# The first chunk of a selective scan, set up by TensorE and VectorE together and evicted tile by tile

## What is computed

```python
def _L1_attn_ref(x, in_proj_w, conv_w, conv_b, x_proj_w, dt_proj_w, dt_proj_b, A_log, D_param, out_proj_w):
    x_in, res = jnp.split(jnp.einsum('bld,ed->ble', x, in_proj_w), 2, axis=-1)
    xp = jnp.pad(x_in, ((0, 0), (K_CONV - 1, 0), (0, 0)))
    conv = conv_b
    for k in range(K_CONV):                                  # 4 taps
        conv = conv + xp[:, k:k + seqlen, :] * conv_w[:, k]
    u = _silu(conv)                                          # 512 channels
    dt_in, Bm, Cm = jnp.split(jnp.einsum('bld,ed->ble', u, x_proj_w), [64, 80], axis=-1)
    dt = jax.nn.softplus(jnp.einsum('blr,er->ble', dt_in, dt_proj_w) + dt_proj_b)
    A = -jnp.exp(A_log)                                      # 512 channels x 16 states
    def step(h, t):
        dt_t, B_t, C_t, u_t = t
        h = jnp.exp(dt_t[:, :, None] * A) * h + (dt_t * u_t)[:, :, None] * B_t[:, None, :]
        return (h, jnp.einsum('bdn,bn->bd', h, C_t))
    ...
    y = (jnp.swapaxes(ys, 0, 1) + u * D_param) * _silu(res)
    return jnp.einsum('blr,or->blo', y, out_proj_w)
```

## Time and profile before

| what | value |
|---|---|
| three runs, median (lowest to highest) | 3345.03 us (3344.44 to 3349.97) |
| the profiled execution's own time | 3345.35 us |
| its span in the trace | 3343.5 us |
| mean granted TensorE clock over the span | 0.966 of full speed |
| TensorE / VectorE / ScalarE / GpSimd busy, share of the span | 90% / 79% / 67% / 67% |
| preparation of chunk 0, from the first instruction of the scan stage to its first scan | 1580.9 to 1625.8 us |

### The profile page before, as it was taken

One profiled execution on the slowest core, in us unless ns is written; L12 is line 12 of the kernel. 1 busy time (PEld: TensorE's weight loads), 2 busy tenths in 40 slices (PEclk: granted clock), 3 DMA queues, 4 the chain that ended last, 5 costly groups with the idle time before them and its releaser, 6 DMA issues. The chain is left out here.

```text
span 3343.5 us, 39386 instructions
## 1 busy us (share of the span) xinstructions
PE 3017.1 (90%) x11504; PEld 1711.8 (51%) x11504; DVE 2644.0 (79%) x3513; ACT 2232.7 (67%) x3411; POOL 2227.2 (67%) x1615
## 2 busy tenths in 40 slices
PE   3589999999999999999889999999988899999997
PEld 1157666666666667777334434433433444444432
DVE  5989989898989898555699999999999444555543
ACT  2457676766767666665566666666564788888886
POOL 3578888888888888776367767776786344444443
PEclk7689999999999999999899999999999999999999
DMA  3034444444444444455122222222321222222222
GB/s 98 13 93 133 125 131 126 120 134 124 125 132 126 122 124 126 142 147 155 48 73 70 73 70 71 72 70 70 92 69 54 90 97 96 103 102 103 102 102 90
DMA packets 199617, 335.38 MB, mean 100 GB/s; under 512 B 21379, under 2 KB 57380, under 8 KB 199020
## 3 DMA queue, kind: packets, MB, share of 16 engines
q1 hardware_dynamic: 199404, 332.86, 32.9%
HBM read 325.69 MB, written 7.09 MB: 100 GB/s over the span
## 5 line engine op out<-in xcount | busy, mean ns | idle before, releaser
L1639 POOL TENSOR_TENSOR c_hc<-c_h,c_c_rep 128x1024 f32<-128x1024 f32 x256 | 604.1, 2360 | 277.0 <-DVE c_h L1681 216.2
L1681 DVE TENSOR_TENSOR_SCAN c_h<-c_decay,c_carry,c_v_ps 128x512 f32<-128x512 f32 x512 | 638.9, 1295 | 0.4 <-DVE c_v_ps L1671 0.4
L2133 POOL TENSOR_TENSOR d_acc<-d_acc,d_prod 128x512 f32<-128x512 f32 x240 | 311.6, 1308 | 421.3 <-DVE d_prod L2201 421.1
L1539 ACT ACTIVATE c_decay<-c_dt,c_a_cols 128x512 f32<-128x512 f32 x512 | 364.0, 721 | 339.2 <-DVE c_h L1681 337.8
L2093 ACT ACTIVATE d_hmid<-d_up,n_b 128x1024 f32<-128x1024 f32 x512 | 532.4, 1118 | 84.9 <-PE d_up L1995 84.7
L1387 PE MATMUL c_y_ps<-c_hc,ident 128*128 128x512 f32 x1024 | 499.2, 611 | 43.5 <-POOL c_hc L1639 31.7
L687 POOL TENSOR_TENSOR ab_inner_low<-ab_inner,ab_inner_high 128x512 fp32r<-128x512 f32 x264 | 341.9, 1295 | 241.1 <-ACT ab_inner_high L570 239.8
L559 ACT ACTIVATE ab_gate_ps<-ab_gate_ps,ab_raw_d 128x512 f32<-128x512 f32 x264 | 174.5, 661 | 430.8 <-PE ab_gate_ps L414 430.7
L2201 DVE SCALAR_TENSOR_TENSOR d_prod<-d_ring,n_b,d_w_rep 128x512 f32<-128x512 f32 x240 | 180.2, 751 | 280.6 <-PE d_ring L2005 145.7
L669 POOL TENSOR_TENSOR ab_hc<-ab_h,ab_c_rep 128x512 f32<-128x512 f32 x256 | 331.8, 1296 | 86.7 <-DVE ab_h L740 65.7
L675 POOL TENSOR_TENSOR ab_gu_low<-ab_raw_gu,ab_gu_high 128x512 fp32r<-128x512 f32 x264 | 341.7, 1294 | 4.3 <-ACT ab_gu_high L546 4.3
(11 more groups left out here) (280 smaller groups left out, 6405.3 us busy)
## 6 DMA issues: line engine op xcount, KB each, us to landing
ab_raw_gu<-in_b_experts SPq DMA_DIRECT2D x264, 256.0 KB, 3.4
ab_w_rep<-ab_w_scratch SPq DMA_DIRECT2D x264, 256.0 KB, 3.6
c_c_rep<-c_c_scratch SPq DMA_DIRECT2D x256, 256.0 KB, 3.1
d_w_rep<-d_w_scratch SPq DMA_DIRECT2D x256, 256.0 KB
ab_raw_d<-in_b_experts SPq DMA_DIRECT2D x264, 129.0 KB, 2.1
ab_raw_x<-in_xT SPq DMA_DIRECT2D x32, 256.0 KB, 4.8
out<-xT SPq DMA_DIRECT2D x8, 512.0 KB, 10.1
xT<-in_xT SPq DMA_DIRECT2D x1, 3072.0 KB, 12.3
```

Source lines behind the costliest of these rows:

```text
L1539: nc.scalar.activation(decay[:, i % DEC, :], dt[:, s, m, :], ACT.Exp, scale=a_cols[:, n * NM + m:n * NM + m + 1]).then_inc(decay_ready, 1)
L1639: nc.gpsimd.tensor_tensor(hc[:, q % HC], h[:, q % HR], c_rep[:, q % BC].unsqueeze(1).broadcast_to([P, PAIR, CH]), ALU.mult).then_inc(hc_re ...
L1681: nc.vector.tensor_tensor_scan(out=h[:, q % HR, m, :], data0=decay[:, i % DEC, :], data1=v_ps[m][:], initial=carry[:, i:i + 1], op0=ALU.mu ...
L2133: nc.gpsimd.tensor_tensor(acc[:, s, g, :], acc[:, s, g, :], prod[:, q % PR, :], ALU.add).then_inc(add_ready, 1)
```

## The change

Only the preparation of chunk 0 is changed, and what the loops need because of it.

- The four projected tiles come in the order 2, 3, 0, 1 and go to four banks (both `v_ps`, `bank_a`, `bank_b`); ScalarE copies each to `xin` as it comes.
- Tiles 2 and 3 are convolved by VectorE in SBUF, straight into `u`: one `tensor_scalar` and three `scalar_tensor_tensor` for each tile, the two tiles alternating, each operation waiting by a semaphore for the one before it on its tile. Tiles 0 and 1 are convolved by TensorE into both `y_ps`. So six banks are in use. The diagonals of tiles 0 and 1 are made first, those of tiles 2 and 3, which chunk 1 is the first to need, after the constants; TensorE's `convolve` of chunk 1 waits for them at tile 2.
- Silu is applied tile by tile, with the convolution's bias: to `u` for tiles 2 and 3, straight from PSUM for 0 and 1. The matmuls of `project_u` follow tile by tile.
- A Softplus of one column into a new tile `spare` comes right behind the last Silu.
- x_dbl is copied before `b_parts`. The four matmuls of dt go to four banks, with no wait between them; Softplus is applied to each straight from PSUM, with its bias.
- The halo copy comes last on ScalarE. After it ScalarE waits for the spare Softplus, the constants (now six) and its own four Softplus, raises five semaphores that the loops count on, and begins the decays.
- VectorE's `dtu` waits for the first two Softplus and the four Silus; the first product waits for all four Softplus.

```diff
             pe.wait_ge(loaded, LOADS)
             pe.sem_inc(y_ready, HC)
+            for n, m in enumerate(FIRST_ORDER):
+                first_x(n, m)
+            pe.wait_ge(diag_ready, 1)
+            for n in range(PAIR):
+                first_convolve(n)
+            first_u()
             for m in range(NM):
-                project_x(0, m)
+                first_dt(m)
             pe.wait_ge(const_ready, CONSTS)
-            for m in range(NM):
-                convolve(0, m, (0, 1, 2, 3))
-            project_u(0, 0, (0, 1, 2, 3))
-            for m in range(NM):
-                project_dt(0, m)
             spread_b(0, 0, 0)
...
+            def first_u():
+                pe.wait_ge(x_left, NM)
+                for n, m in enumerate(FIRST_ORDER):
+                    pe.wait_ge(first_u_ready, n + 1)
+                    done = nc.tensor.matmul(bank_b[:], x_w[:, m, :], u[:, 0, m, :],
+                                            start=(n == 0), stop=(n == NM - 1))
+                done.then_inc(xd_ready, 1)
...
+            act.wait_ge(halo_ready, 1)
+            for n, m in enumerate(FIRST_ORDER):
+                act.wait_ge(x_ready, n + 1)
+                nc.scalar.copy(xin[:, m, HALO:], (v_ps[0], v_ps[1], bank_a, bank_b)[n][:]).then_inc(x_left, 1)
+            for n, m in enumerate(FIRST_ORDER):
+                if n < PAIR:
+                    act.wait_ge(first_cv, n + 1)
+                    src = u[:, 0, m, :]
+                else:
+                    act.wait_ge(cv_ready, n - PAIR + 1)
+                    src = y_ps[m][:]
+                nc.scalar.activation(u[:, 0, m, :], src, ACT.Silu, bias=conv_b[:, m:m + 1]).then_inc(first_u_ready, 1)
+            nc.scalar.activation(spare[:, 0:1], conv_b[:, 0:1], ACT.Softplus).then_inc(spare_ready, 1)
+            act.wait_ge(xd_ready, 1)
+            nc.scalar.copy(x_dbl[:], bank_b[:]).then_inc(xd_left, 1)
+            nc.scalar.copy(b_parts[RANK:, 0, :], bank_b[RANK:, :]).then_inc(xd_left, 1)
             for m in range(NM):
-                leave_x(0, m)
+                act.wait_ge(dtp_ready, m + 1)
+                nc.scalar.activation(dt[:, 0, m, :], (v_ps[0], v_ps[1], bank_a, bank_b)[m][:], ACT.Softplus,
+                                     bias=dt_b[:, m:m + 1]).then_inc(dt_half_ready, 1)
+            nc.scalar.copy(xin[:, :, 0:HALO], xin[:, :, CH:CH + HALO]).then_inc(halo_ready, 1)
+            act.wait_ge(spare_ready, 1)
             act.wait_ge(const_ready, CONSTS)
-            for m in range(NM):
-                leave_conv(0, 0, m)
-            keep_halo(0)
-            activate_u(0, 0)
-            leave_x_dbl(0, 0)
-            leave_dt(0, 0, 0)
...
-            softplus(0, 0, 0, 1)
-            softplus(0, 0, 1, 1)
+            act.wait_ge(dt_half_ready, NM)
+            act.sem_inc(dt_ready, PAIRS)
+            act.sem_inc(dtp_left, NM)
+            act.sem_inc(cv_left, NM)
+            act.sem_inc(cv_ready, PAIR)
+            act.sem_inc(u_ready, 1)
...
+            def first_convolve():
+                dve.wait_ge(halo_ready, 1)
+                dve.wait_ge(x_left, PAIR)
+                for j in range(TAPS):
+                    for m in FIRST_ORDER[:PAIR]:
+                        at = FIRST_ORDER.index(m)
+                        if j == 0:
+                            nc.vector.tensor_scalar(u[:, 0, m, :], xin[:, m, 0:CH], conv_w[:, m, 0:1], None,
+                                                    ALU.mult).then_inc(first_step[at], 1)
+                        else:
+                            dve.wait_ge(first_step[at], j)
+                            nc.vector.scalar_tensor_tensor(
+                                out=u[:, 0, m, :], in0=xin[:, m, j:j + CH], scalar=conv_w[:, m, j:j + 1],
+                                in1=u[:, 0, m, :], op0=ALU.mult, op1=ALU.add
+                            ).then_inc(first_cv if j == TAPS - 1 else first_step[at], 1)
...
             nc.vector.memset(xin[:, :, 0:HALO], 0.0).then_inc(halo_ready, 1)
+            diagonals((0, 1)).then_inc(diag_ready, 1)
             nc.vector.memset(carry[:], 0.0).then_inc(const_ready, 1)
...
+            first_convolve()
             nc.vector.memset(b_parts[0:RANK].bitcast(F32), 0.0).then_inc(const_ready, 1)
...
             nc.vector.tensor_scalar(a_cols[:], a_cols[:], -1.0, None, ALU.mult).then_inc(const_ready, 1)
+            diagonals((2, 3)).then_inc(diag_ready, 1)
             dve.wait_ge(const_ready, CONSTS)
...
             nx.place_embedding(dve)
-            first_input()
+            ms = slice(0, PAIR)
+            dve.wait_ge(dt_half_ready, PAIR)
+            dve.wait_ge(first_u_ready, NM)
+            nc.vector.tensor_tensor(dtu[:, ms], dt[:, 0, ms], u[:, 0, ms], ALU.mult).then_inc(dtu_ready, 1)
+            dve.wait_ge(dt_half_ready, NM)
```

More of the change, by code:

```diff
@@ L1177, in layer1_scan @@
         carry = sb("carry", [P, NT])
+        spare = sb("spare", [P, 8])
         z = sb("z", [P, 2, CH])
@@ L1191, in layer1_scan @@
         const_ready = sem("const_ready")
+        diag_ready = sem("diag_ready")
+        first_cv = sem("first_cv")
+        first_u_ready = sem("first_u_ready")
+        first_step = [sem(f"first_step{i}") for i in range(PAIR)]
         x_ready = sem("x_ready")
@@ L1284, in convolve @@
                 if taps[0] == 0:
+                    if is_int(r, 1) and m == 2:
+                        pe.wait_ge(diag_ready, 2)
                     if m < 2:
@@ L1437, in chunk, with first_x, first_convolve, first_dt @@
                         add_states(c, q - 2)
+            def first_x(n, m):
+                out = (v_ps[0], v_ps[1], bank_a, bank_b)[n]
+                for half in range(2):
+                    done = nc.tensor.matmul(out[:], in_w[:, half, m * P:(m + 1) * P], xT[:, half, 0:CH],
+                                            start=(half == 0), stop=(half == 1))
+                done.then_inc(x_ready, 1)
+            def first_convolve(m):
+                pe.wait_ge(x_left, PAIR + m + 1)
+                for j in range(TAPS):
+                    done = nc.tensor.matmul(y_ps[m][:], conv_diag[:, m, j, :], xin[:, m, j:j + CH],
+                                            start=(j == 0), stop=(j == TAPS - 1))
+                done.then_inc(cv_ready, 1)
+            def first_u():
[5 more added lines that the diff above has]
+                done.then_inc(xd_ready, 1)
+            def first_dt(m):
+                if m == 0:
+                    pe.wait_ge(xd_left, 2)
+                out = (v_ps[0], v_ps[1], bank_a, bank_b)[m]
+                nc.tensor.matmul(out[:], dt_w[:, m * P:(m + 1) * P], x_dbl[0:RANK, :],
+                                 start=True, stop=True).then_inc(dtp_ready, 1)
             pe.wait_ge(loaded, LOADS)
             pe.sem_inc(y_ready, HC)
+            for n, m in enumerate(FIRST_ORDER):
[4 more added lines that the diff above has]
+            first_u()
             for m in range(NM):
-                project_x(0, m)
+                first_dt(m)
             pe.wait_ge(const_ready, CONSTS)
-            for m in range(NM):
-                convolve(0, m, (0, 1, 2, 3))
-            project_u(0, 0, (0, 1, 2, 3))
-            for m in range(NM):
-                project_dt(0, m)
             spread_b(0, 0, 0)
@@ L1741, in chunk, with diagonals @@
                     scan(c, q, 1)
+            def diagonals(ms):
+                for m in ms:
+                    for j in range(TAPS):
+                        done = nc.vector.tensor_scalar(conv_diag[:, m, j, :], k["ident"], conv_w[:, m, j:j + 1], None,
+                                                       ALU.mult)
+                return done
+            def first_convolve():
+                dve.wait_ge(halo_ready, 1)
+                dve.wait_ge(x_left, PAIR)
+                for j in range(TAPS):
+                    for m in FIRST_ORDER[:PAIR]:
[9 more added lines that the diff above has]
+                            ).then_inc(first_cv if j == TAPS - 1 else first_step[at], 1)
             dve.wait_ge(loaded, LOADS)
             nc.vector.memset(xin[:, :, 0:HALO], 0.0).then_inc(halo_ready, 1)
+            diagonals((0, 1)).then_inc(diag_ready, 1)
             nc.vector.memset(carry[:], 0.0).then_inc(const_ready, 1)
[L1746 to L1749, removed]
-            done.then_inc(const_ready, 1)
+            first_convolve()
             nc.vector.memset(b_parts[0:RANK].bitcast(F32), 0.0).then_inc(const_ready, 1)
```

13 lines of the change are left out of this document (4 added, 9 removed).

## The result

The changed kernel took 3328.3 us (median of five runs, 3327.86 to 3330.16), the kernel before 3349.97 us over five runs beside it (3344.44 to 3360.31). The ratio on record is 0.9939, with a 95% interval of 0.9924 to 0.9954; it is an estimate from the runs and not the quotient of the two medians, which is 0.9935. Two of the five runs of the kernel before, at 3360.1 and 3360.3, stand 10 us or more above the other three, so the difference of these two medians, 21.7 us, is more than the profiles bear out. The profiled execution took 3327.86 us, 17.5 us less than that of before (3345.35). It holds all three numbers that the case turns on: where the first scan starts, how long the stage runs from there, and how long the last stage takes.

The account below looks back on a forecast made before the run. VectorE bounds the scan stage but idles 28.58 us before it, behind a ScalarE and TensorE chain. Bringing the first scan 18.6 us earlier takes 3345.35 to 3326.7 (3326.4 from the median); forecast 3326.5 us, range 3323 to 3331.

Parts of the forecast that it names:

- TensorE up to x_dbl: Chunk 0's preparation, projections through two convolutions and x_w: x_dbl copied at 1598.6 instead of 1614.49, 15.9 us earlier.
- Beside it: Work beside TensorE before x_dbl: VectorE's convolution 4.8 us, Silu load and Silus, constants, embedding; Silus ready in time, costing nothing.
- The rival that VectorE becomes the bound: VectorE's eight convolution operations each expose a 0.49 us semaphore round trip: 2.1 us less gained, 3328.6 us; chance 10%.
- dt and the tail: From x_dbl to the first scan: Softplus done at 1604.3, then 0.8 and 2.1 us; first scan 1607.2, 18.6 us earlier.
- the clock rival: TensorE's clock falls to 0.50 after its pause between x_w and dt: 3.4 us lost, 3330 us; chance 10%.
- The tail of 0.8 us: ScalarE after the last Softplus: halo copy 0.2 us, three waits and five semaphore counts 0.6 us (bounds 0 to 1.0).
- The table loads: ScalarE's function-table loads take 1.28 us each without a drain; two off the chain are worth 2.56 of the 18.6 us.
- Moves with it: From the first scan on, VectorE never lacks work, so stage end and what follows come earlier by as much.
- The slower rival: TensorE stays behind through all 256 scan steps, 0.12 us each costing 29 us, net 3356 us; chance 2%.
- The base: Kernel before: the sum used its profiled execution, 3345.35 us, 0.3 us above the median of three runs, 3345.03.

Follow-up runs that it names:

- pe_all: Changed kernel with all four tiles of chunk 0 convolved by TensorE into four banks, all diagonals made first; 3340.79 us, single profiled execution.
- split_consts: Kernel before, with TensorE's convolutions waiting for the diagonals alone and the other constants waited for later; 3342.14 us, single profiled execution.
- u_late: Changed kernel with TensorE's x_w waiting for all four Silus before its first matmul; 3332.25 us, single profiled execution.
- dve_serial: Changed kernel with VectorE convolving tile 2 wholly, then tile 3, instead of alternating; 3327.47 us, single profiled execution.
- no_spare: Changed kernel without the one-column spare Softplus and the wait for it; 3327.84 us, single profiled execution.
- leave_early: Changed kernel with ScalarE copying chunk 1's projected tiles in chunk 0's steps 1, 3, 5, 7 instead of 5 to 8; 3332.61 us, single profiled execution.
- again: Changed kernel measured once more with no edit; median 3331.99 us, ratio 0.9956 to the kernel before.
- again2: Changed kernel measured a third time with no edit; median 3329.63 us, ratio 0.9945 to the kernel before.

## Why the prediction was right

The forecast was 3326.5 us, range 3323 to 3331, and 3328.3 was measured; the gain between the profiled executions was forecast at 18.6 us and was 17.5. The mechanism came as forecast: the first scan starts earlier by what the chain up to it loses, 17.83 us for a forecast 18.6, and the rest moves with it. That the total came within 1.8 us is in part luck, as the same code had medians of 3328.3, 3332.0 and 3329.6 in three comparisons, of which 3332.0 lies outside the range. Nor is the first scan at 1607.48, forecast at 1607.2, as close as it looks: from the stage's start it was 27.03 for 26.3.

- **TensorE up to x_dbl.** Forecast 17.7 us after the stage's start, measured 17.61 or 17.62 in all ten profiles that leave this part as it is. Against the first copy before, at 33.57, that is 15.96 us (forecast 15.9). Parts of it were taken out one by one: two convolutions 6.87 (pe_all), the wait for constants 2.3 and part of the clock 0.87 (split_consts), the order of x_w 1.1 (u_late). About 4.8 us are left, of which the rest of x_w's slow clock is 1.6 (x_w to its copy takes 3.63 instead of 6.08); the remainder, Silu tile by tile out of PSUM and no eviction or halo between, is argued, as no run undoes it alone.
- **Beside it.** VectorE's 4.8 us were 4.86, the Silu load started straight behind the last copy. VectorE's wait ahead of `dtu`, forecast at 1 us, was gone, as one group of eight small casts took 1.72 us where its like took 0.73 before; the room behind it bore that. The rival that VectorE becomes the bound fell with dve_serial.
- **dt and the tail.** This is the step that was mis-sized. The first Softplus was at 20.01 (forecast 20.1), the last started at 23.73 instead of 22.7: the clock rival, priced at 3.4 us for a fall ahead of dt, came true in part, in the middle of it, and cost 1.14. I had given it 10%; in ten profiles with the pause unaltered it was there in five, so 10% was far too little. What sets the fall stays open. My reason against it, that a 2.0 us pause kept the clock, was one case of one phase. The tail of 0.8 us was 0.50 (3.30 less 0.69 and the 2.1 of load, decay and signal).
- **The table loads.** That the loads take 1.28 us and no drain held. That the spare Softplus takes one off the chain did not: without it the load hides elsewhere, for 0.1 us (no_spare). So of the 2.56 us that I gave the two loads, the spare column earned 0.1.
- **From the first scan on.** "Moves with it" was right to 0.2 us for the scan stage and 1.0 for the last one in this profile, but the same code ranges from 970.84 to 972.51 and from 746.15 to 754.62 us there. The slower rival, a TensorE late through all 256 steps, did not come; its lag is ten steps long and starts with copies placed too late (leave_early).
- **The base.** The kernel before, 3345.03 in the three runs shown, had medians of 3347.6 and 3348.7 over nine runs in two later comparisons. Against those the gain is 15.6 us (again) and 19.1 (again2), and against the three runs it is 16.7. So the forecast of 18.6 holds within some 3 us, and no better than that.

## What to carry to other kernels

Where one engine never idles in a stage, time the instruction that starts it, count everything from the stage's own start, and sum only the chain up to that instruction: here that gave the first scan's move, 17.83 us, to within 0.8. Undo the parts one at a time, since a part can be hidden by its neighbour (the spare Softplus). And read a fall of TensorE's clock from several executions of the same code before it is put down to an edit: one profile each is not enough for effects of a microsecond.

## What the runs showed that I had not expected

- A pause of 1.28 us, with matmuls of 64 rows behind it, was followed by a fall of the granted clock to 0.50 in five profiles of ten, 2.3 to 2.7 us after TensorE had taken up work again and while it was busy. In the other five the clock stayed at 1.00 through dt and fell in the first steps of the scan.
- What the clock spares in one place it can take in the next: again2 gained 1.14 us in dt and lost 1.7 from the first scan on, 1.4 of it around chunk 1's x_w; leave_early, which removed ten late steps, ended 3.1 us longer. This agrees with what the Trainium skill says of the monitor (TensorE: Matmul & The Clock Gate, What's actually happening), that it runs freely. The same code with two outcomes, again and again2, is this case's sign of it, and no proof.
- A multiply-add of 128x512 in SBUF on VectorE that waits for the one just before it costs about 0.13 us more than one that waits for the one before that (0.75 us over six, dve_serial).
